# A decoder layer on one core: three buffers for split terms, and extremes that GpSimd folds two columns to one

## The reference

```python
x = _layernorm(x + _L0_attn_ref(x, ...))              # 16 heads of 8, softmax over 128 keys
x = _layernorm(x + _L0_xattn_ref(ctx_1024, x, ctx_1024, ...))   # the same form, keys and values from ctx
x = _layernorm(x + _L0_ffn_ref(x, W1, b1, W2, b2))    # 128 -> 512 -> 128
```

```python
amin, amax = (jnp.min(x), jnp.max(x))
scale = jnp.maximum((amax - amin) / 255.0, 1e-08)
zp = jnp.clip(jnp.round(-amin / scale) + QMIN, QMIN, QMAX)
q = jnp.clip(jnp.round(x / scale) + zp, QMIN, QMAX)
```

## Time and profile before

| | |
|---|---|
| Times of three runs | 335.9, 337.71 (median), 339.79 us |
| The profiled execution | 336.97 us, its span 335.2 us |
| Busy share of the span | DVE 92%, PE 80%, ACT 74%, POOL 59% |
| Attention, until the last maximum | to about 245 us |
| Extremes of x2 and the rest of the attention | about 246 to 263 us |
| Feed-forward up to the extremes of h | about 263 to 307 us |
| Second quantisation, second product, last norm | about 307 to 335 us |

### The profile page before, as it was taken

One profiled execution on the slowest core, in us unless ns is written; L12 is line 12 of the kernel. 1 busy time (PEld: TensorE's weight loads), 2 busy tenths in 40 slices (PEclk: granted clock), 3 DMA queues, 4 the chain that ended last, 5 costly groups with the idle time before them and its releaser, 6 DMA issues.

```text
span 335.2 us, 12397 instructions
## 1 busy us (share of the span) xinstructions
PE 268.9 (80%) x4917; PEld 168.2 (50%) x4917; DVE 306.8 (92%) x705; ACT 248.1 (74%) x502; POOL 196.8 (59%) x397
## 2 busy tenths in 40 slices
PE   4678989799999999999999988798885267416981
PEld 3355656566666666566566655555553123102551
DVE  5668899899999999999999999889989779998995
ACT  2246889688988889888888887768773299910995
POOL 2856788887667676666666846855322113901395
PEclk9999999999999999999999999989998575757896
DMA  2452424244242342424423232321100000000026
GB/s 64 115 151 85 115 77 127 59 129 116 73 122 69 113 125 64 128 59 116 118 63 114 83 113 81 107 73 52 30 3 0 1 2 0 0 0 0 2 63 189
DMA packets 48992, 25.13 MB, mean 75 GB/s; under 512 B 6440, under 2 KB 48808, under 8 KB 48936
## 3 DMA queue, kind: packets, MB, share of 16 engines
q1 hardware_dynamic: 46504, 23.74, 24.5%
q10 hardware_dynamic: 2432, 0.60, 0.8%
HBM read 9.39 MB, written 2.10 MB: 34 GB/s over the span
## 4 chain that ended last, share of the span: by engine, by line
DVE 41%; POOL 24%; issue 19%; PE 6%; SPq 4%; DMA 3%; ACT 2%; POOLq 1%; DVEq 0%; ACTq 0%
DVE neg_max L944 15%; DVE h_ext L1060 5%; DVE h_ext L1061 5%; POOL rstd L587 5%; SPq L438 3%; DVE arena_q L1087 2%; POOL arena_h L615 2%; POOL var_eps L584 2%; DVE arena_q L936 2%; POOL parts_ck L405 2%; PE ps L1188 2%; POOL parts_cq L405 2%; DVE o_stats L1096 2%; POOL parts_cq L403 2%; POOL parts_ck L403 2%
## 5 line engine op out<-in xcount | busy, mean ns | idle before, releaser
L944 DVE TENSOR_REDUCE neg_max<-ps 128x8 f32<-128x1024 f32 x128 | 157.1, 1227 | 10.4 <-PE ps L1188 10.0
L768 ACT ACTIVATE probs<-ps 128x1024 f32<-128x1024 f32 x64 | 65.5, 1024 | 22.8 <-PE ps L1195 22.8
L759 ACT ACTIVATE probs<-ps 128x1024 f32<-128x1024 f32 x64 | 65.6, 1024 | 16.3 <-PE ps L1195 12.8
L1188 PE MATMUL ps<-arena_h 31*128 31x128 f16 x1024 | 52.4, 220 | 21.1 <-DVE neg_max L944 11.2
L1188 PEld LDWEIGHTS ps<-arena_h 31*128 31x128 f16 x1024 | 30.6, 94 | 55.6 <-DVE neg_max L944 38.3
L1195 PE MATMUL ps<-arena_h 32*128 32x128 f16 x1024 | 51.3, 217 | 0.6 <-ACT probs L768 0.6
L584 POOL TENSOR_TENSOR var_eps<-mean_var,eps_col 128x1 f32<-128x1 f32 x64 | 12.3, 192 | 65.8 <-DVE mean_var L928 65.8
L1216 PE MATMUL ps<-probs,arena_h 128*32 128x128 f32 x1024 | 42.3, 282 | 0.2 <-issue 0.2
L1216 PE MATMUL ps<-probs,arena_q 128*32 128x128 f32 x1024 | 41.2, 279 | 0.0
L587 POOL TENSOR_TENSOR rstd<-var_eps,minus_half 128x1 f32<-128x1 f32 x64 | 35.3, 551 | 5.2 <-POOL var_eps L584 0.3
L1195 PEld LDWEIGHTS ps<-arena_h 32*128 32x128 f16 x1024 | 29.3, 93 | 1.5 <-ACT probs L768 1.0
(11 more groups left out here) (168 smaller groups left out, 618.0 us busy)
## 6 DMA issues: line engine op xcount, KB each, us to landing
arena_h<-parts_sq SPq DMA_DIRECT2D x48, 64.0 KB, 1.9
arena_h<-parts_ck SPq DMA_DIRECT2D x48, 64.0 KB, 2.3
arena_h<-parts_cq SPq DMA_DIRECT2D x48, 64.0 KB, 2.1
arena_h<-parts_sk SPq DMA_DIRECT2D x46, 64.0 KB, 2.0
xT_in<-in_xT_dram SPq DMA_DIRECT2D x16, 128.0 KB, 2.4
xN_in<-in_xN_dram SPq DMA_DIRECT2D x16, 128.0 KB, 2.3
cT_in<-in_cT_dram SPq DMA_DIRECT2D x16, 128.0 KB, 2.5
cN_in<-in_cN_dram SPq DMA_DIRECT2D x16, 128.0 KB, 2.4
```

What stands on the lines that cost most here:

```text
L759: act.activation(probs[1][:, :], ps_s2, ACT.Exp, scale=SCALE).then_inc(ex, 1)
L768: act.activation(probs[0][:, :], ps_s2, ACT.Exp, scale=SCALE).then_inc(ex, 1)
L944: dve.tensor_reduce(neg_max[b.par][:, HH * half:HH * half + HH], ps_s1.rearrange("p (h k) -> p h k", h=HH), AXX, ALU.max, negate=True).the ...
L1188: ins = pe.matmul(ps_s1[:, at:at + S], q[r:r + MAX_AT, j, :], kk[r:r + MAX_AT, j, :], start=True, stop=True, skip_group_check=True)
```

## The change

1. `parts` has three buffers instead of two, and `split` waits for the transfers of pair i - 3. `cq_pairs` uses another condition: the pairs 12 and 13 are now split in the slots 48 and 50 instead of 49 and 51, all others stay.
2. The three transfers that fill cq of pair 0 go from SP's queue to ACT's, in slot 8.
3. POOL folds: for 14 of the 16 pairs of cross outputs it writes the greater and the smaller of two sequences, element by element (`fold`: subtract, clip at 0, add, subtract, with two semaphore waits in between, which the profile also shows as gaps). The folds lie at the end of POOL's slots 20, 24, ... 56, then 60, 61, 63 and 64. DVE reduces 4, 4, 4 and 2 folded pairs and then the last two pairs as before: six pairs of reductions instead of nine.
4. POOL instead of DVE normalises the tasks at positions 58 to 61.
5. POOL folds the halves of the units 3, 6, 9 and 12 of h (512 columns against 512), and DVE reduces 512 columns of each, in another order of units.
6. PE computes ten more unread products around the first `share_extremes`.

```diff
+PARTS = 3
...
-EXT_AT = [(4 * i, 4) for i in range(B // 4 - 1)] + [(B - 4, 2), (B - 2, 2)]
-NEXT = len(EXT_AT)
-EXT_SLOTS = {TASKS - 2: (0, 1), TASKS - 1: (2, 3), TASKS: (4, 5), TASKS + 1: (6,), TASKS + 2: (7,)}
+FOLDED_PAIRS = 14
+EXT_FOLDED = [(0, 4), (4, 4), (8, 4), (12, 2)]
+EXT_AT = [(B - 4, 2), (B - 2, 2)]
+NEXT = len(EXT_FOLDED) + len(EXT_AT)
+EXT_SLOTS = {TASKS - 2 + i: i for i in range(NEXT - 1)}
+
+FOLDED_UNITS = (3, 6, 9, 12)
+EXTREMES_ORDER = (1, 2, 4, 5, 3, 7, 8, 6, 10, 11, 9, 13, 14, 12, 15)
...
+def by_pool(t):
+
+    return TASKS - 6 <= t.pos < TASKS - 2
...
+def fold_pair(k):
+
+    for i in range(FOLDED_PAIRS):
+        if k == (C_POS[2 * i] + 8 if i < PAIRS - LEAD_PAIRS + 1 else C_POS[2 * i] + 7 if i < FOLDED_PAIRS - 1 else TASKS):
+            return i
+    return None
...
-    free = [C_POS[2 * (i - 2)] - FILL_AT + 1 if i > 1 else FIRST_SLOT for i in range(PAIRS)]
+    free = [C_POS[2 * (i - RING)] + 2 if i >= RING else FIRST_SLOT for i in range(PAIRS)]
...
-            if i > 1:
-
-                eng.wait_ge(*stacks_landed(name, i - 2))
+            if i >= PARTS:
+
+                eng.wait_ge(*stacks_landed(name, i - PARTS))
...
+            def fold(a, b, diff, over, larger, smaller, done):
+
+                pool.tensor_tensor(diff, a, b, ALU.subtract).then_inc(fold_step, 1)
+                pool.wait_ge(fold_step, folds[0] + 1)
+                pool.tensor_scalar(over, diff, 3.0e38, 0.0, ALU.min, ALU.max).then_inc(fold_step, 1)
+                folds[0] += 2
+                pool.wait_ge(fold_step, folds[0])
+                pool.tensor_tensor(larger, b, over, ALU.add)
+                pool.tensor_tensor(smaller, a, over, ALU.subtract).then_inc(done, 1)
...
+                i = fold_pair(k)
+                if i is not None:
+                    need(pool, xn, made_to(C_POS[2 * i + 1], False))
+                    need(pool, xc, made_to(C_POS[2 * i + 1], True))
+                    fold(x2_all[:, 2 * i, :], x2_all[:, 2 * i + 1, :], fold_diff[:, :], fold_over[:, :],
+                         x2_max[:, i, :], x2_min[:, i, :], xf)
+                for v in crosses:
+                    pool.wait_ge(rq, v.pos + 1)
+                    pool.tensor_scalar(x2_all[:, v.m, :], y_sb[v.place][:, :], minus_mean[v.par][:, :], rstd[v.place][:, :],
+                                       ALU.add, ALU.mult).then_inc(xc, 1)
...
+            x_ints(2)
+            x_ints(3)
+            fold_unit(0)
+            x_ints(4)
+            fold_unit(1)
...
+            x2_bias(0)
+            fold_unit(2)
+            x2_bias(1)
+            fold_unit(3)
+            x2_bias(2)
+            x2_bias(3)
...
+                if 0 in cq_pairs(k):
+                    act.wait_ge(c_cleared, 1)
+                    act.wait_ge(split_done["cq"], 1)
+                    for t, part in enumerate(Q_PARTS):
+                        act.dma_start(stack["cq"][0][t::ROW_STEP, :, :],
+                                      parts["cq"][0][:, part, :]).then_inc(stacks_landed("cq", 0)[0], 16)
...
-            for u in range(1, NU):
+            for u in EXTREMES_ORDER:
                 c, hc = divmod(u, NHC)
-                h_extremes(u + 1, hT[:, hc, c * CH:(c + 1) * CH])
+                if u in FOLDED_UNITS:
+                    n = FOLDED_UNITS.index(u)
+                    dve.wait_ge(f_fold, n + 1)
+                    h_extremes(u + 1, *[y_out[2 * (n % 2) + m][:, :, :].rearrange("p b d -> p (b d)") for m in range(2)])
...
+            pe.wait_ge(w_ints, 2)
+            pe.wait_ge(mx, 2 * TASKS)
+            unread_products(6)
             share_extremes(0)
-            pe.wait_ge(w_ints, 2)
+            unread_products(4)
```

More of the change, by code:

```diff
@@ L231, in decoder_layer @@
         cq_full = [sb(f"cq_full{i}", [128, PAIR]) for i in range(RING)]
-        parts = {n: [sb(f"parts_{n}{i}", [128, 2, PAIR], F16) for i in range(2)] for n in NAMES}
+        parts = {n: [sb(f"parts_{n}{i}", [128, 2, PAIR], F16) for i in range(PARTS)] for n in NAMES}
         words = HQ * PAIR // 2
@@ L644, in _, with x_ints @@
             over_slots(slot)
-            for i in range(DVE_PIECES, NP):
+            def x_ints(i):
                 n = PIECES[i][1]
@@ L912, in x2_extremes @@
             def x2_extremes(i):
[L913 to L917 removed]
+                if i < len(EXT_FOLDED):
+                    first, count = EXT_FOLDED[i]
+                    larger, smaller = x2_max[:, first:first + count, :], x2_min[:, first:first + count, :]
+                    dve.wait_ge(xf, first + count)
+                else:
+                    first, count = EXT_AT[i - len(EXT_FOLDED)]
+                    larger = smaller = x2_all[:, first:first + count, :]
+                    dve.wait_ge(xn, made_to(C_POS[first + count - 1], False))
+                    need(dve, xc, made_to(C_POS[first + count - 1], True))
+                dve.tensor_reduce(x2_ext[:, 0, i:i + 1], larger, AX2, ALU.max).then_inc(mm, 1)
+                dve.tensor_reduce(x2_ext[:, 1, i:i + 1], smaller, AX2, ALU.min, negate=True).then_inc(mm, 1)
             def slot(k):
@@ L998, in slot @@
                         new_x(t)
[L999 to L1000 removed]
+                if k in EXT_SLOTS:
+                    x2_extremes(EXT_SLOTS[k])
             over_slots(slot)
@@ L1353, in share_extremes, with unread_products @@
                           skip_group_check=True).then_inc(f_all, 1)
+            def unread_products(count):
+                for _ in range(count):
+                    pe.matmul(bank(0), w1_q[:, 0:128], w2_q[:, :], start=True, stop=True)
+            pe.wait_ge(w_ints, 2)
+            pe.wait_ge(mx, 2 * TASKS)
+            unread_products(6)
             share_extremes(0)
-            pe.wait_ge(w_ints, 2)
+            unread_products(4)
             turn_x(0)
@@ L1370, in _ @@
                     turn_x(c + 2)
-            def unread_products(count):
-                for _ in range(count):
-                    pe.matmul(bank(0), w1_q[:, 0:128], w2_q[:, :], start=True, stop=True)
             pe.wait_ge(f_g, NU + 1)
```

73 lines of the change are left out of this document (51 added, 22 removed).

## The result

The changed kernel took **332.27 us** in the median of 12 runs (331.5 to 334.64), the kernel before 337.29 us beside it (12 runs, 335.15 to 341.7). The ratio of the two is 0.9863, with a 95% interval of 0.9838 to 0.9889. The profiled execution took 331.59 us, its span 329.9; before it was 336.97 and 335.2. That is 5.4 us between the profiled executions, where 5.9 were forecast; the two medians differ by 5.0.

The account below looks back on a forecast made before the run. DVE was taken as the longest chain, busy 39.98 of 40 us in steady attention. Terms summed to -5.9 from 336.97: 331.1, or 331.8 against the median; forecast 331.5 us between them, range 328.5 to 334.3.

Parts of the forecast that it names:

- third buffer: Late attention: POOL's two waits for ck transfers and DVE's two following waits go; -2.0 us, between -2.0 and 0.
- first fill of cq on ACT: First cross scores: earlier transfers remove most of DVE's 1.52 us wait but delay ACT; -0.3 us, between -1.5 and +0.5.
- folds of x2 in the attention: Slots 20 to 48: DVE's normalisation waits 0.15 us for POOL's third fold step in eight slots; +1.2 us, 0 to +4.2.
- end of the attention: After the last maximum: fewer DVE reductions and normalisations save 4.7 us, new waits cost 1.6; -3.1 us, -4.5 to -2.0.
- unread products: Before the first shared extremes: PE kept busy, so the wait for the shared value shrinks; -0.3 us, between 0 and -0.7.
- folds of h: Feed-forward reductions: DVE saves 4.2 us, less 2.8 of waits (0.7, 1.0, 1.2); -1.4 us, between -4.2 and +0.5.
- Rival A: Attention: POOL's folds hold DVE out for their last two steps, 0.53 us in eight slots; 334.5 us, chance 0.12.
- Rival C: Attention: the fold drags each course of four slots, DVE waits for scores; slower, up to 343.5 us, chance 0.05.
- Rival D: Late attention: a third buffer gives nothing, because the ring place held the fills back; 333.5 us, chance 0.11.
- Rival B: First cross scores and feed-forward: ACT's delay stays hidden (-1.2) and POOL folds faster (-1.5); 328.8 us, chance 0.12.

## Why the prediction was right, point by point

| term | forecast | in the traces |
|---|---|---|
| third buffer | -2.0 | -1.9 (undone: 148.39 against 146.53) |
| first fill of cq on ACT | -0.3 | -0.2 and -0.3 (12.27 and 12.36 to 12.03 and 12.06) |
| folds of x2 in the attention | +1.2 | +0.8 without DVE's idle time (145.67 against 144.82) |
| end of the attention | -3.1 | -3.2 |
| unread products | -0.3 | -0.6 and -0.2 |
| folds of h | -1.4 | -1.5 and -1.6 |
| last stage | not counted | +0.7 and +0.6 |

The time, 332.27, lies 0.8 us above the forecast of 331.5 and inside its range; the sum of -5.9 compares to -5.4, between the two second traces to -6.2, and between the medians to -5.0. Part of this agreement is luck. From slot 8 to the last maximum the forecast has -1.1 in all, and the traces have -2.1 and -2.0. The last stage, at +0.7 and +0.6, was not in the sum, and in the first pair of traces the start came 1.2 us later, which is scatter. Without these two the gain would have been 7.4 and 6.9 us, a microsecond or more above the forecast.

**The method held where one engine is the longest chain without a gap.** In the feed-forward the walk through POOL's and DVE's orders gave three waits, 0.7, 1.0 and 1.2; they were 0.64, 0.80 and 1.02. The mechanism held as well at the end of the attention, but its -3.1 is a sum of two errors that cancel. The change added waits of 0.5, 0.8 and 0.3 by the forecast; it added 0.41 and 0.63, and DVE's whole idle time there grew by 1.1 (1.44 to 2.59). And the work that went from DVE was not 4.7 but 4.3 us: the four normalisations are worth 0.4 and not 0.7, since three reciprocals and the `att` that reads each now stand nearly as far apart without them (0.29, 0.29 and 0.28 us from start to start, where it was 0.59 with two normalisations between them and 0.33 with one).

**POOL's prices were low by a little.** A step of two different inputs at 128 columns takes 0.46 us; the 0.40 that I took is of a row that adds a broadcast zero. The fold is 1.80 us, not 1.67. At 512 columns 1.27 against 1.24. Three starts of cq keep ACT for 1.89 us and not 1.6.

**Rival A fell.** The normalisation met the third step as computed, and where it did DVE got in before the fourth, though POOL's two steps follow without a gap: 0.58 instead of the 0.87 that A gives. In slot 24 it came so late in the third step that the fourth held it instead, for as long (0.57). No normalisation in any trace was held by both. Rival C fell too: the long stretch is 0.8 us longer with the folds, less than DVE's own stalls. Rival D fell with the two-buffer kernel. Rival B fell by the 1.46 us in slot 9. The first fill's mechanism came as foretold, one wait put in the place of another one slot earlier. Its size of -0.3 was a choice between bounds and no sum, and it agrees with the two pairs of traces by luck: the average over more traces is nearer to a loss of 0.6 than to a gain of 0.3. That is not resolved in the times.

**What was not counted.** The last stage is 0.6 to 0.7 us longer. Laid beside each other, the first traces of before and after differ by 0.20 at the second shared value (a wait of 0.67 against 0.47, with PE's granted clock at 0.70 from 300 to 304 us, where it was 0.83 from 306 to 310 before), by 0.24 at one `o_stats` in the first pieces, and by 0.30 in the landing of the last output. The first goes with the clock: between 0.8 and 1.7 us after the reduction of `h_ext` it was granted at 0.50 in the changed kernel, the level of 1.2 GHz, and at 1.00 before. Of the twelve traces of the changed kernel and its variants nine have this wait at 0.67 or 0.68, with a clock of 0.50 to 0.66, and three at 0.47 or 0.48, with 0.82 to 1.00; the last stage of these three is 28.55 to 28.57. The second is in that one trace alone. The third is in all: the last transfer of the output landed 2.37 and 2.31 us after its start in the two traces of before and 2.65 to 2.67 in the twelve. It writes the same 256 KB from the same queue, and why it lands later is open.

The start scatters: slot 8 began between 51.95 and 54.42 us in fourteen traces, more than any part but the end of the attention is worth. The traces show it as waits of DVE for PE between 20 and 54 us whose lengths differ (in the two that began at 54.16 and 54.01 slot 8's own first maximum waited 1.54 and 1.44); what makes PE late there is open.

## What to carry to other kernels

Helper work on a second engine costs nothing by its own time only as long as it ends before its reader comes, as the waits of 0.80 and 1.02 for the folds of h show, and it costs its collisions in any case: before giving POOL a step, list which `tensor_scalar` and element-wise instructions of DVE will run beside it, above all short ones on the path such as `top_diag`, and move the step beside a reduction. When a wait is removed by moving transfers to another queue, count three starts of 0.6 us as work of that queue's engine, and ask whether the wait is a landing time that varies. And walk through both engines' orders unit by unit: it gave waits to 0.2 us here, and it would have shown that the fourth fold earns nothing.

## What the runs showed of the hardware

The hold of a DVE `tensor_scalar` behind a POOL step depends on what is left of POOL's step, not on DVE's own length: 0.24 us more behind one of 0.46 that had begun just before, 1.85 more behind one of 2.3, for four elements. It ends 0.26 us before the recorded end of the POOL step in the attention (99.69 + 0.58 - 0.34 = 99.93, with POOL's end at 100.19), and 0.20 us before it for `top_diag` (303.19 - 0.22 = 302.97, POOL's end 303.17). And POOL does not hold DVE over two of the fold's steps, though they follow without a gap. In slot 40's timeline DVE comes 0.11 us after the third step's start, waits 0.09 and is at work from about 170.73, the fourth step starting at 170.94 in its record:

```profile
170.53 0.46 POOL L617 TENSOR_TENSOR arena_h<-x_all,arena_h 128x128 f32<-128x128 f32 x1
170.64 0.43 DVE L1036 TENSOR_SCALAR arena_q<-y_sb,mean_var,rstd 128x128 f32<-128x128 f32 x1
170.94 0.46 POOL L618 TENSOR_TENSOR arena_h<-x_all,arena_h 128x128 f32<-128x128 f32 x1
```

In slot 24 it comes 0.08 us before the third step's recorded end, and is at work only from 114.19 + 0.57 - 0.34 = 114.42, again 0.26 before a recorded end, but that of the fourth step (114.68):

```profile
113.81 0.46 POOL L617 TENSOR_TENSOR arena_h<-x_all,arena_h 128x128 f32<-128x128 f32 x1
114.19 0.57 DVE L1036 TENSOR_SCALAR arena_q<-y_sb,mean_var,rstd 128x128 f32<-128x128 f32 x1
114.22 0.46 POOL L618 TENSOR_TENSOR arena_h<-x_all,arena_h 128x128 f32<-128x128 f32 x1
```

Both read as if POOL's steps lay a quarter of a microsecond earlier than their records against DVE's. This is shown for the fold's steps alone: the row of clears in the earlier trace rows held a normalisation over all of its steps, for 2.08 us.

The Trainium skill (SBUF — State Buffer, Who interferes with whom) has the other engine fully blocked for a whole instruction. By that rule the normalisation in slot 20 waits to 100.19 and the one in slot 40 to 170.99; the rows show 99.93 and 170.73. The rule names the right pairs and the right size; the recorded end lies a quarter of a microsecond behind the release.
